# One scatter-add ahead of two row fetches on GpSimd, and one transpose ahead of its neighbour's matmuls on TensorE

## The reference

```
x = x + L0_xattn(layernorm(x), ctx)     # one-head attention over the context
x = x + L0_ffn(layernorm(x))            # slot routing, top 8 of 64, a GRU step on the slots
x = x + L1_xattn(layernorm(x), ctx)     # 16 heads, then a relu layer
x = x + L1_ffn(layernorm(x))            # 8 experts, each token uses 2
```

```
scores = softmax(x @ gate_w.T)                     # 8 experts in 4 groups, 2 groups are kept
topk_ids, topk_w = _grouped_topk(scores)           # 2 experts, weights sum to 1
gate, up = x @ w13[e].T                            # 2 x 512
out += topk_w[e] * (silu(gate) * up) @ w2[e].T     # for both experts e of the token
```

## Time and profile before

| | us |
|---|---|
| median of 3 runs | 564.83 |
| lowest and highest | 564.78, 565.56 |
| the profiled execution | 564.83 |
| its span, first to last instruction | 563.0 |
| TensorE busy | 539.2 (96%) |
| VectorE busy | 294.4 (52%) |
| ScalarE busy | 243.8 (43%) |
| GpSimd busy | 168.2 (30%) |

### The profile page before, as it was taken

One profiled execution on the slowest core, in us unless ns is written; L12 is line 12 of the kernel. 1 busy time (PEld: TensorE's weight loads), 2 busy tenths in 40 slices (PEclk: granted clock), 3 DMA queues, 4 the chain that ended last, 5 costly groups with the idle time before them and its releaser, 6 DMA issues.

```text
span 563.0 us, 11051 instructions
## 1 busy us (share of the span) xinstructions
PE 539.2 (96%) x3954; PEld 443.6 (79%) x3955; DVE 294.4 (52%) x875; ACT 243.8 (43%) x560; POOL 168.2 (30%) x152
## 2 busy tenths in 40 slices
PE   9999999999999999999999789999999999999990
PEld 8788878767555777777767678889999999999990
DVE  6748778878453867757688866741111111111110
ACT  1333666262456677778786343222222222222210
POOL 3102000103132232232112052444345444454432
PEclk9999999999999999999999999999999999999996
DMA  8930000001010000300641937687878787877621
GB/s 326 395 114 1 2 1 1 1 1 38 0 38 0 2 2 2 112 3 2 230 182 33 347 126 252 203 251 216 244 217 263 216 261 222 250 231 241 189 34 19
DMA packets 28507, 74.15 MB, mean 132 GB/s; under 512 B 5584, under 2 KB 20176, under 8 KB 23216
## 3 DMA queue, kind: packets, MB, share of 16 engines
q1 hardware_dynamic: 14368, 57.66, 28.8%
q0 software_dynamic: 7488, 10.39, 9.4%
q10 hardware_dynamic: 6608, 5.54, 3.0%
HBM read 62.86 MB, written 10.72 MB: 131 GB/s over the span
## 4 chain that ended last, share of the span: by engine, by line
PE 61%; DMA 21%; DVE 5%; issue 5%; ACT 3%; DVEq 1%; POOLq 0%; ACTq 0%; POOL 0%
PE ps L858 43%; DMA out_x<-arena,row_no 21%; PE ps L862 9%; PE ps L1150 4%; PE ps L1011 1%; PE ps L1002 1%; PE ps L1014 1%; ACT ring L587 1%; PE ps L942 1%; DVE mx L1649 1%; PE ps L1005 1%; PE ps L985 1%; DVE heads_out L1663 1%; ACT arena L536 1%; DMA keep<-early,row_no 1%
## 5 line engine op out<-in xcount | busy, mean ns | idle before, releaser
L858 PE MATMUL ps<-keep,arena 128*128 128x128 f32 (+2 forms) x976 | 114.5, 274 | 0.2 <-DVE arena L1583 0.2
L858 PEld LDWEIGHTS ps<-keep,arena 128*128 128x128 f32 x976 | 112.4, 192 | 1.6 <-DVE arena L1583 0.8
L1958 DVE TENSOR_TENSOR keep<-keep,ps 128x512 f32<-128x512 f32 x39 | 26.8, 687 | 146.3 <-PE ps L858 128.6
L392 POOL DMA_INDIRECT out_x<-arena,row_no x39 | 61.4, 1574 | 107.6 <-DMA out_x<-arena,row_no 52.1
L1150 PE MATMUL ps<-arena,keep 128*128 x312 | 73.9, 380 | 1.0 <-issue 1.0
L356 POOL TENSOR_TENSOR ring<-arena,keep 128x512 f32<-128x512 f32 x32 | 33.3, 1041 | 103.5 <-PE ps L858 98.5
L1150 PEld LDWEIGHTS ps<-arena,keep 128*128 128x128 f32 x312 | 56.3, 190 | 7.5 <-issue 1.5
L627 ACT COPY keep<-ps 128x256 f32<-128x256 f32 x39 | 14.5, 372 | 102.8 <-PE ps L862 102.8
L587 ACT ACTIVATE ring<-ps,mx 128x128 f32<-128x128 f32 x192 | 52.3, 405 | 7.1 <-DVE mx L1649 4.6
L858 PE MATMUL ps<-ring,arena 128*32 128x128 f32 (+1 forms) x640 | 53.5, 349 | 0.9 <-ACT ring L594 0.8
L348 POOL TENSOR_TENSOR var_x<-var_x,minus_half 128x4 f32<-128x4 f32 x16 | 16.5, 1031 | 94.0 <-DVE var_x L1505 94.0
(11 more groups left out here) (259 smaller groups left out, 809.5 us busy)
## 6 DMA issues: line engine op xcount, KB each, us to landing
arena<-in_w SPq DMA_DIRECT2D x29, 1024.0 KB
w_first<-in_w SPq DMA_DIRECT2D x10, 1024.0 KB
arena<-in_w SPq DMA_DIRECT2D x8, 512.0 KB, 7.2
keep<-in_keep SPq DMA_DIRECT2D x1, 3099.0 KB, 21.1
ring<-in_fold SPq DMA_DIRECT2D x1, 2112.0 KB, 12.3
arena<-in_x SPq DMA_DIRECT2D x4, 512.0 KB, 10.4
arena<-in_ctxT SPq DMA_DIRECT2D x4, 512.0 KB, 7.5
out_x<-arena ACTq DMA_DIRECT2D x4, 512.0 KB, 3.3
```

The source lines that it names most:

```text
L392: pool.indirect_dma_start(out=out_d, out_offset=bass.IndirectOffsetOnAxis(ap=row_no[:, t:t + 1], axis=0), in_=YO[t % DEEP], in_offset=None ...
L858: ins = pe.matmul(out, w, m, start=(k == 0), stop=(k == len(pairs) - 1))
L1958: dve.tensor_tensor(HA[r % 2], HA[r % 2], ps[:, 2 * (r % 2) + 1, :], ALU.mult).then_inc(act_ok, 1)
```

## The change

Two rows of the orders written by hand move. On GpSimd `add(5)` is issued ahead of `fetch(9)` and `fetch(10)`. On TensorE `turn_in(9)` stands ahead of `gate_up(8)`. Nothing else differs.

```diff
             add(3)
             add(4)
+            add(5)
             fetch(9)
             fetch(10)
-            add(5)
             fetch(11)
...
             turn_in(0, 8)
             down(0, 6)
+            turn_in(0, 9)
             gate_up(0, 8)
-            turn_in(0, 9)
             down(0, 7)
```

## The result

| | before | changed |
|---|---|---|
| median of 4 runs, us | 565.19 | 570.75 |
| lowest and highest, us | 564.78, 565.7 | 569.88, 571.29 |
| span of the profiled execution, us | 563.0 | 568.3 |
| mean granted clock over the span | 0.992 | 0.987 |

The ratio is 1.0099, with a 95% interval from 1.0086 to 1.0111: 5.6 us slower, where 3.3 were forecast and 5.3 was the end of the range. The sign and the place were right. The price was too low.

What follows compares the result with a forecast made beforehand. TensorE, without idle time in the loop, was taken to set the end, with adds behind it. Its 3.7 us shift, less what the catching-up adds give back, made plus 3.3 us on 564.83: 568.1 us, range 566.7 to 570.1.

Steps and rivals of the forecast that it cites:

- What bounds the kernel: Expert-tile loop: TensorE has no idle time, adds run behind it, so its shift reaches the end almost whole.
- Fetch 9 starts at 377.5: GpSimd: behind add 5, which waits for add 4's landing, fetch 9 starts at 377.5 instead of 373.78.
- It lands at 381.1: Landing of fetch 9: taken as 381.1, between the two contended values 380.73 and 381.55.
- The upper bound: Landing of fetch 9: only where the DMA engines' full stretch ends, at 381.55; TensorE's shift then 4.1 us.
- TensorE's shift, landing less 377.44: TensorE from `down(7)` on: later by fetch 9's landing less 377.44, taken as 3.7 us.
- The clock: TensorE behind the stall: granted clock may fall, slowing half of `gate_up(8)`, 1.8 us; chance 0.18, outside the sum.
- The end: Last adds: add 37 starts 0.75 us after its answer instead of 1.1, so the span ends 3.3 us later.
- The kept lag: Adds behind TensorE: lag stays, so everything shifts by the full 3.7 us, to 568.5 us; chance 0.12.
- Add 6 one us later at no cost: GpSimd: add 6 starts near 384.0, about 1 us later, costed at nothing because TensorE's own delay is larger.
- The clock's case: TensorE behind the stall: half of `gate_up(8)` at slow clock adds 1.8 us, giving 569.9 us; chance 0.18.
- The short stall: Fetch 9: add 4 done earlier, landing at 379.6, TensorE's shift 2.2 us, 566.7 us; chance 0.08.
- the held cover: Fetch 9: lands by 377.4 while TensorE waits for ScalarE anyway, no stall, 564.4 us; chance 0.03.

Runs made afterwards that it cites:

- e3_both_filled: Both rows moved, plus eight matmuls on zeros ahead of `turn_in(9)` to fill TensorE's wait, against the kernel before: ratio 1.0064.
- e5_fetch_delayed: TensorE's row moved, GpSimd's order as before but waiting for add 4 to land ahead of fetch 9, against the kernel before: ratio 1.0082.
- e7_changed_again: Both rows moved, the changed kernel unaltered and profiled a second time, against the kernel before: ratio 1.0095.
- e4_weights_later: Both rows moved, and the weights of tile 11 loaded one tile later, against the kernel before: ratio 1.0068.
- e2_turn_only: TensorE's row alone moved, GpSimd's order as before, against the kernel before: ratio 1.0009.
- e1_add_only: GpSimd's row alone moved, TensorE's order as before, against the kernel before: ratio 1.0021.

## Why the prediction was wrong in size

**What bounds the kernel.** Right. TensorE is busy for all of 389 to 533 us after as before, and its shift reached the end, less what the adds gave.

**Fetch 9 starts at 377.5.** In the changed kernel's two traces it started at 375.24 and 378.38. The rule behind it was right (add 5 waits for the landing of add 4): the working put 5.3 us between the starts of the two adds, and they were 5.2 to 5.6 in four traces and 6.1 in the first. Its input varies: add 4 started at 367.26 in the first trace and from 370.34 to 371.61 in all others, and with 370.35 in e3_both_filled fetch 9 started at 377.77. So the changed kernel's first trace is the odd one. Why its add 4 was early isn't known.

**It lands at 381.1.** It landed at 381.04 and 382.63. The first is a hit by luck: the fetch started 2.3 us earlier than forecast and took 5.80 us where 3.6 were taken, and the two errors cancel. The sum put the landing 3.2 to 4.0 us after the start, where it goes with the load of weights. The upper bound, which tied it to the full stretch of the engines, had the better reason.

**TensorE's shift, landing less 377.44.** Right as far as it goes: 381.04 gives 3.6 us, and 3.7 were forecast. In e3_both_filled, where the clock held, TensorE took up the transposes at 381.74, `gate_up(8)` followed them 0.44 us later and took 3.57 us, as the working had it.

**The clock.** This is the step that failed. The forecast gave it 0.18 and left it out of the sum, "may or may not meet such a fall". It fell in both traces of the changed kernel, and the mean granted clock of all its other executions was 0.987 to 0.989, beside 0.991 to 0.994 in the executions of before. The row that the argument used said as much: at the end of the kernel the clock had fallen 3.3 us after the last matmul, and the stall that the prediction forecast was 4.5 us. The likeliest case should have been that it falls. Its price was also too low, 1.8 us, since half of `gate_up(8)` was taken for slow and nothing of the transposes. About two thirds of the one and all of the other were: 5.91 and 0.69 us instead of 3.57 and 0.44, **2.6 us**. With it the sum is 3.6 + 2.6 - 0.9 = 5.3 us, which is the difference of the two spans (the medians differ by 5.6).

**The end.** Add 37 was to start 0.75 us after its answer. It started 0.27 us after it (555.59 - 555.32). The 0.75 us was taken from a start behind a landing, and a start behind an answer is shorter. So the adds gave back 0.9 us and not 0.4. The kept lag, which had a chance of 0.12, occurs as well: add 37 started 0.27 us after its answer in e5_fetch_delayed, 0.57 in e3_both_filled, 1.11 in e7_changed_again and 1.21 in e4_weights_later.

**Add 6 one us later at no cost.** It started at 383.46 and 385.06, and the adds were at their answers by tile 7 in both. Right.

**The rivals.** The clock's case gave 569.9 us and was 0.9 us short of the measured 570.75. The short stall and the held cover did not occur with both rows; e2_turn_only shows what the held cover looks like, with GpSimd's old order.

## What to carry to other kernels

When two small reorderings meet at one transfer, look for the work that covered it: here one row moved a fetch 1.4 to 3.6 us later, by TensorE's own position, and the other moved its reader 3.8 us earlier, at 1.2 and 0.5 us alone and 5.6 us together. If the stall that you forecast for TensorE is longer than the idle time after which the trace shows its clock falling, the slow clock belongs in the sum and not among the rivals. And look for the next bulk load before you delay a small fetch, because here a fetch that started beside it landed 5.5 to 6.2 us after the load's issue whenever it had started itself, and one that started 2 us ahead of the load had landed 1.9 us after the issue at the latest.

## What the runs showed of the hardware that was not expected

The time from the last matmul to the fall of the granted clock isn't fixed. It was 3.3 us at the end of the kernel before, 3.0 us in the first trace of the changed kernel (376.71 to about 379.7), 3.6 us in e5_fetch_delayed and 4.4 us in the second trace (377.66 to about 382.1). In e4_weights_later it was near 4.4 us, too, and there TensorE had been at work again for 0.9 us when the clock fell. In e3_both_filled an idle time of 1.35 us left the clock alone. In the windows of e7_changed_again the clock is back at 1.00 by 386:

```profile
381.75:382.25 0.50, 0.00 (x0) 0.00 (x0) 0.00 (x0) 0.00 (x0) 0.20 (x2) 0.84 0.66 232
382.25:386.00 3.75, 3.32 (x18) 3.33 (x19) 0.33 (x2) 0.00 (x0) 2.81 (x3) 0.57 0.40 113
386.00:387.00 1.00, 1.00 (x12) 1.00 (x11) 0.00 (x0) 0.73 (x2) 0.67 (x1) 1.00 0.01 4
```

The time at the low level differed, too: 6.8 us in the first trace and in e5_fetch_delayed, 3.4 us in e4_weights_later and in e7_changed_again. So a stall of 3.4 to 5.0 us cost 1.3 to 2.9 us of slow matmuls behind it (`gate_up(8)` with its transposes: 5.34 us in e7_changed_again, 6.90 us in e5_fetch_delayed, 4.01 us at full clock), and the longest stall cost the least.

A matmul queue that ran dry for 0.12 us cost 1.0 us in e1_add_only: 0.12, 0.22, 0.41 and 0.26 us. The largest piece, 0.41 us, stands ahead of `down(7)`, whose first step is the load of an expert number into a register. That the register load is what shows there is likely from the code and was not tried.
